# A decoder layer on one core: last batch's end, multiplications of ones in TensorE's waits, half loads, sums on TensorE, and one ring of banks

## The reference

```python
x = x + mla_attention(layernorm(x))     # 16 heads, low-rank q (192) and kv (64), rope of 64, causal
x = x + quantized_expert(layernorm(x))  # SmoothQuant int8 gate/up and down, weights given per batch
x = x + moe(layernorm(x))               # 32 experts, top 4 of 3 of 8 groups, 40 slots each, and a shared expert

def _smooth_quant_linear(x, w):
    s = sqrt(max(amax_x, EPS) / max(amax_w, EPS))        # by column
    x_scale, w_scale = rowmax(|x / s|) / 127, rowmax(|w * s|) / 127
    return round(x / s / x_scale) @ round(w * s / w_scale).T * x_scale * w_scale.T

# moe: a slot is kept when its place in its expert's queue is below C = 40
Yf = Y.reshape(EC, d) * slots_w[:, None]
out = zeros((T, d)).at[slots_token].add(Yf)
```

## Time and profile before

| | |
|---|---|
| median of 3 runs | 391.88 us (391.5 to 392.9) |
| profiled execution | 394.86 us, span 393.0 us, mean clock of TensorE 0.953 |
| TensorE busy | 320.9 us, 82% |
| VectorE busy | 258.6 us, 66% |
| ScalarE busy | 171.5 us, 44% |
| GpSimd busy | 101.3 us, 26% |
| chain that ended last | PE 46%, DVE 22%, issue 12%, ACT 8%, POOL 7%, DMA 4% |

### The profile page before, as it was taken

The page is one execution under the profiler, slowest core; times in us unless marked ns, Lnnn a source line. Parts: engine busy times, 40 slices in busy tenths (PEclk is TensorE's granted clock), DMA queues, the critical chain, the costliest instruction groups (busy, mean ns, idle before and its releaser), DMA issues.

```text
span 393.0 us, 6471 instructions
## 1 busy us (share of the span) xinstructions
PE 320.9 (82%) x1960; PEld 222.9 (57%) x1960; DVE 258.6 (66%) x1058; ACT 171.5 (44%) x536; POOL 101.3 (26%) x144
## 2 busy tenths in 40 slices
PE   1899998899998878998798899777697571699890
PEld 0555665566866656765465676555585461455580
DVE  2347776676488868867897879785596590143527
ACT  1225576756547665336584716654033100134200
POOL 4121222221031102035422014331015416015700
PEclk9999999999999999998999999989989877599996
DMA  7999691020000000000000000153000000545165
GB/s 263 337 407 366 219 387 51 0 81 2 2 2 0 3 1 0 3 5 34 6 3 5 3 0 2 35 181 115 0 2 3 16 2 2 139 133 206 32 239 201
DMA packets 17894, 34.25 MB, mean 87 GB/s; under 512 B 4780, under 2 KB 9513, under 8 KB 17220
## 3 DMA queue, kind: packets, MB, share of 16 engines
q1 hardware_dynamic: 15556, 32.64, 23.7%
q0 software_dynamic: 2304, 1.20, 1.1%
HBM read 27.08 MB, written 11.99 MB: 99 GB/s over the span
## 4 chain that ended last, share of the span: by engine, by line
PE 46%; DVE 22%; issue 12%; ACT 8%; POOL 7%; DMA 4%; POOLq 0%; DVEq 0%; another core or an unknown queue 0%; SPq 0%; ACTq 0%
PE psum L522 37%; PE psum L531 9%; POOL expert_rows L1574 2%; DVE x_residual L1491 2%; DVE region_t L1159 2%; ACT region_t L918 1%; POOL token_parts L1585 1%; ACT region_r L866 1%; DVE region_t L1167 1%; DMA region_a<-token_parts 1%; DMA x_residual<-in_x_dram 1%; ACT region_t L916 1%; DVE region_t L1157 1%; POOL rstd L1536 1%; DVE bn_stats L1057 1%
## 5 line engine op out<-in xcount | busy, mean ns | idle before, releaser
L522 PE MATMUL psum<-region_h,region_b 128*128 128x256 f32 (+1 forms) x320 | 66.9, 347 | 2.9 <-DVE region_b L1471 1.8
L522 PE MATMUL psum<-region_c,region_h 128*128 128x512 f32 x128 | 62.2, 610 | 2.1 <-ACT q_chunk L866 1.1
L916 ACT ACTIVATE region_t<-region_t,neg_max 128x128 f32<-128x128 f32 x64 | 25.6, 401 | 67.3 <-DVE neg_max L1159 65.6
L522 PEld LDWEIGHTS psum<-region_h,region_b 128*128 128x128 f32 x320 | 48.2, 194 | 11.1 <-issue 5.5
L1548 POOL TENSOR_TENSOR q_chunk<-q_chunk,q_rope_tmp 128x256 f32<-128x256 f32 x32 | 23.4, 733 | 97.7 <-DVE q_chunk L1138 97.6
L1574 POOL DMA_INDIRECT expert_rows<-h_moe,slot_scatter x32 | 33.2, 1037 | 24.1 <-DVE slot_scatter L1403 16.2
L531 PE MATMUL psum<-consts,region_t 128*128 128x128 f32 x192 | 32.5, 278 | 7.6 <-DVE region_t L1167 4.5
L522 PEld LDWEIGHTS psum<-region_c,region_h 128*128 128x128 f32 x128 | 23.1, 194 | 20.3 <-issue 17.2
L531 PEld LDWEIGHTS psum<-consts,region_t 128*128 128x128 f32 x192 | 22.9, 142 | 20.4 <-issue 13.0
L918 ACT ACTIVATE region_t<-region_t,neg_max 128x256 f32<-128x256 f32 x64 | 31.6, 494 | 0.0
L522 PE MATMUL psum<-region_t,region_h 128*64 128x256 f32 (+1 forms) x256 | 27.8, 340 | 2.9 <-ACT region_t L866 2.9
(11 more groups left out here) (185 smaller groups left out, 603.5 us busy)
## 6 DMA issues: line engine op xcount, KB each, us to landing
region_a<-in_experts_dram SPq DMA_DIRECT2D x17, 384.0 KB, 6.2
region_b<-in_experts_dram SPq DMA_DIRECT2D x10, 384.0 KB, 6.6
region_a<-in_fold_dram SPq DMA_DIRECT2D x3, 1152.0 KB, 13.2
token_parts<-region_g SPq DMA_DIRECT2D x12, 256.0 KB, 5.8
region_a<-token_parts SPq DMA_DIRECT2D x6, 512.0 KB, 6.2
region_c<-in_experts_dram SPq DMA_DIRECT2D x5, 384.0 KB, 3.2
expert_rows<-region_g SPq DMA_DIRECT2D x10, 132.5 KB, 10.6
region_h<-expert_rows SPq DMA_DIRECT2D x5, 256.0 KB, 3.8
```

What stands on the lines that cost most here:

```text
L522: return nc.tensor.matmul(out_, lhsT, rhs, start=first, stop=last)
L916: nc.scalar.activation(pr[:, 0:P], pr[:, 0:P], ACT.Exp, bias=nmax[:, hn, 0:1], scale=-1.0, accum_out=sums[:, hn, 0:1])
```

## The change

- `FILL`: TensorE multiplies a 128x128 bf16 matrix of ones by itself, into the bank of the step that follows, 20 times before x_T.3, 30 before x_back.3, 40 before x_back2.3, 140 before xpT.0. The wait for the empty bank comes first; the wait for the data comes behind the ones. The rows of the last batch are still scattered and loaded.
- The end: each tile's parts are loaded in two halves (256 KB), even tiles by SyncE, odd tiles by ScalarE; stores are divided in the same way. Tiles 4 and 5 are no longer combined on VectorE: `weigh` makes 8 matrices, the identity times a token weight, and `sum` multiplies them with the parts on TensorE, four f32 matmuls of 128x256 a tile; VectorE adds the sum to the residual.
- `inv_ready` comes in two halves, xs and then ws, and `x_back` has 6 parts and not 4.
- The `q` projections lose their own bank; the ring of the attention stage is banks 4 to 7 for all.
- The whole `ORDER` is written anew. Up to `tail` the same steps stand in a similar order; behind it the part below.

```diff
-BANK_S, BANK_PT, BANK_O, BANK_Q, BANK_W = 0, 2, 3, 4, 5
+BANK_S, BANK_PT, BANK_O, BANK_W = 0, 2, 3, 4
+FILL = {("x_T", 3): 20, ("x_back", 3): 30, ("x_back2", 3): 40, ("xpT", 0): 140}
 ORDER, from the step behind `tail` on, new:
+y_first.7 tail y_last.6 y_last.7 y_add.6 y_add.7 x_stats.3 x_stats.3+1 r_logit.2 r_groups.2 r_groups.2+1
+r_groups.2+2 x_norm.3 r_groups.2+3
+r_groups.2+4 r_groups.2+5 r_best.2 x_T.3 x_T.3+1 r_best.2+1 r_best.2+2 r_best.2+3 r_best.2+4 r_best.2+5
+x_smooth.3 x_smooth.3+1 r_choose.2 r_choose.2+1 r_choose.2+2 x_smooth.3+2 r_choose.2+3 r_weights.2 s_gate.0
+s_up.0 s_silu.0 r_weights.2+1 x_scale.3 x_back.3 r_weights.2+2 r_weights.2+3 x_back.3+1 r_weights.2+4 s_mul.0
+s_gate.1 x_back.3+2 x_back.3+3 x_back.3+4 s_down.0 r_weights.2+5 r_pos.2 x_back.3+5 s_silu.1 x_qscale.3
+x_round.3 x_qT.3 scatter.2.0 r_slots.2 r_slots.2+1 r_slots.2+2 r_slots.2+3 x_mm.3 x_tanh.3 r_slots.2+4 x_gate.3
+s_up.1 x_gate.3+1 x_gate.3+2 x_gate.3+3 x_smooth2.3 x_smooth2.3+1 x_smooth2.3+2 x_scale2.3 scatter.2.1
+scatter.2.2 x_back2.3 scatter.2.3 scatter.2.4 scatter.2.5 x_back2.3+1 x_back2.3+2 s_add.0 s_mul.1 x_qscale2.3
+s_gate.2 x_round2.3 x_qT2.3 x_mm2.3 x_mm2.3+1 x_mm2.3+2 s_down.1 scatter.2.6 scatter.2.7 r_stats.3 r_stats.3+1
+s_add.1 r_norm.3 s_silu.2 s_up.2 s_mul.2 r_T.3 r_logit.3 r_groups.3 r_groups.3+1 r_groups.3+2 r_groups.3+3
...
+scatter.3.0 s_down.3 xpT.0 scatter.3.1 scatter.3.2 s_add.2 s_mul.3 xpT.1 s_add.3 gate_up.0 scatter.3.3
+scatter.3.4 scatter.3.5 scatter.3.6 gate_up.1 gate_up.2 hidT.0 hidT.1 xpT.2 xpT.3 scatter.3.7 slot_weights
+down.0 gate_up.3 gate_up.4 hidT.2 hidT.3 down.1 down.2 gate_up.5 onehot.0 xpT.4 hidT.4 down.3 gate_up.6 down.4
+hidT.5 gate_up.7 onehot.1 onehot.2 onehot.3 onehot.4 onehot.5 onehot.6 onehot.7 down.5 hidT.6 down.6 hidT.7
+down.7 onehot.8 onehot.9 onehot.10 onehot.11 onehot.12 onehot.13 onehot.14 onehot.15 weigh.0 combine.0 mix.6
+combine.2 mix.7 sum.4 sum.5
@@ SyncE
-            for t in range(SCATTERED):
-                sp.dma_start(parts[:, t, :], pv[t]).then_inc(ld_parts[t], 16)
+            for t in range(0, SCATTERED, 2):
+                for half in range(2):
+                    c0 = half * TOPK * D // 2
+                    sp.dma_start(parts[:, t, c0:c0 + TOPK * D // 2], pv[t][:, c0:c0 + TOPK * D // 2]
+                                 ).then_inc(ld_parts[half][t], 16)
@@ TensorE
+            def busy(item, n):
+                for _ in range(n):
+                    mm(bank(item)[:, 0:P], ones_bf[:], ones_bf[:])
...
+                    wait_empty(pe, step)
+                    busy(step, FILL.get(step, 0))
                     pe.wait_ge(ld_rows[i], 16)
...
+                elif kind == "sum":
+                    t, = a
+                    pe.wait_ge(sg["weigh_ready"], 1)
+                    wait_empty(pe, step)
+                    for k in range(TOPK):
+                        if k % 2 == 0:
+                            pe.wait_ge(ld_parts[k // 2][t], 16)
+                        last = mm(bank(step)[:, 0:D], weigh[:, SUMMED.index(t), k, :], parts[:, t, k * D:(k + 1) * D],
+                                  k == 0, k == TOPK - 1)
+                    fills(last, step)
@@ VectorE
+                elif kind == "weigh":
+                    dve.wait_ge(sg["token_weights_ready"], B)
+                    wait_filled(dve, ("dn", NG_E - 1))
+                    for i, t in enumerate(SUMMED):
+                        for k in range(TOPK):
+                            last = v.tensor_scalar(weigh[:, i, k, :], ident, wtok[:, t, k:k + 1], None, ALU.mult)
+                    last.then_inc(sg["weigh_ready"], 1)
```

More of the change, by code:

```diff
@@ L100 @@
[L100 to L114, removed]
@@ L145 @@
-s_gate.0 x_scale.3 r_choose.2+3 r_weights.2 r_weights.2+1 r_weights.2+2 s_up.0 s_silu.0 x_back.3 x_back.3+1
-r_weights.2+3 r_weights.2+4 x_back.3+2 x_back.3+3 x_qscale.3 r_weights.2+5 r_pos.2 scatter.2.0 s_gate.1 s_mul.0
-r_slots.2 x_round.3 r_slots.2+1 r_slots.2+2 s_down.0 s_add.0 x_qT.3 x_mm.3 r_slots.2+3 r_slots.2+4 x_tanh.3
-x_gate.3 x_gate.3+1 x_gate.3+2 x_gate.3+3 s_silu.1 x_smooth2.3 x_smooth2.3+1 x_smooth2.3+2 s_up.1 s_mul.1
-scatter.2.1 scatter.2.2 scatter.2.3 scatter.2.4 s_gate.2 x_scale2.3 scatter.2.5 scatter.2.6 x_back2.3
@@ L150 @@
-x_back2.3+1 x_back2.3+2 s_down.1 x_qscale2.3 x_round2.3 s_silu.2 s_add.1 x_qT2.3 x_mm2.3 scatter.2.7 x_mm2.3+1
-x_mm2.3+2 r_stats.3 s_up.2 r_stats.3+1 r_norm.3 r_T.3 r_logit.3 s_mul.2 r_groups.3 r_groups.3+1 r_groups.3+2
-s_down.2 r_groups.3+3 r_groups.3+4 r_groups.3+5 r_best.3 r_best.3+1 r_best.3+2 r_best.3+3 r_best.3+4 r_best.3+5
-r_choose.3 r_choose.3+1 r_choose.3+2 r_choose.3+3 r_weights.3 r_weights.3+1 r_weights.3+2 r_weights.3+3 s_gate.3
-r_weights.3+4 r_weights.3+5 r_pos.3 r_slots.3 r_slots.3+1 r_slots.3+2 r_slots.3+3 r_slots.3+4 s_up.3 s_silu.3
@@ L155 @@
-scatter.3.0 s_down.3 s_mul.3 s_add.2 s_add.3 scatter.3.1 scatter.3.2 scatter.3.3 scatter.3.4 scatter.3.5
-scatter.3.6 xpT.0 xpT.1 gate_up.0 xpT.2 scatter.3.7 gate_up.1 hidT.0 gate_up.2 hidT.1 down.0 slot_weights xpT.3
-gate_up.3 hidT.2 down.1 gate_up.4 hidT.3 down.2 xpT.4 gate_up.5 hidT.4 down.3 gate_up.6 hidT.5 down.4 onehot.0
-onehot.1 onehot.2 onehot.3 gate_up.7 hidT.6 down.5 onehot.4 onehot.5 onehot.6 onehot.7 hidT.7 down.6 onehot.8
-onehot.9 onehot.10 onehot.11 down.7 onehot.12 onehot.13 onehot.14 onehot.15 combine.0 mix.6 combine.2 mix.7
@@ L196 @@
     "xpT": [("xpT", 1)], "gate_up": [("gu", 1)], "hidT": [("hidT", 1)], "down": [("dn", 1)],
-    "mix": [("mix", 1)],
+    "mix": [("mix", 1)], "sum": [("sum", 1)],
 }
@@ L948, in _ @@
                     b, = a
-                    act.wait_ge(sg["inv_ready"], b + 1)
                     if b >= 1:
```

174 lines of the change are left out of this document (105 added, 69 removed).

## The result

The changed kernel took 400.13 us (median of 4 runs, 398.15 to 401.81) beside 392.39 us for the kernel before (4 runs, 391.5 to 393.52): ratio 1.0194, 95% interval 1.0124 to 1.0263. The forecast was 388.5, range 385.2 to 392.4, so it is wrong in sign; what happened has the place and nearly the size of rival D. The profiled execution took 401.79 us, span 400.0, against 394.86 and 393.0 before.

What follows compares the result with a forecast made beforehand. TensorE bounds attention, a serial chain the last batch's steps, TensorE the experts, then scatters, loads and VectorE the end. Terms -3.0 - 1.0 + 0.9 - 0.4 - 0.3 + 0.4 = -3.4 from 391.88 gave 388.5 us, range 385.2 to 392.4.

Steps and rivals of the forecast that it cites:

- rival D: Attention: new order sets dependent steps closer and starves TensorE; slower from +5.8 us of gaps, 395 at +7; chance 0.1.
- Attention: 22 to 262 us, shared ring and rewritten order: TensorE's gaps change little, +0.4 us, bounds -3 to +5.
- the other terms: All but attention: end -3.0, ones -1.0, cross step +0.9, router -0.4, experts' order -0.3 us.
- pairs of probsT: Attention: pairs with nothing between them cost 0.74 us each and rise from 5 to 7.
- q's wait: Attention: the separate bank of q cost one wait of 1.1 us, which can go.
- The end: Combine and sum: half loads and TensorE sums let VectorE end at 387.7, not 390.79; -3.0 us, bounds -1.3 to -4.0.
- The 140 ones: Before xpT.0: ones end about 3 us before the rows and partly save the experts' clock; -1.0 us, bounds 0 to -2.5.
- Cross step and router: Last batch: moved steps and ones outweigh clock gains in the cross step, +0.9 us; r_logit.3 at full clock, -0.4 us.
- the split of the reciprocals: Cross step: inv_ready in halves should scale xs early, but moved steps intervene; +0.7 us.
- The experts' order: Experts: 14 scatters in a row on GpSimd end at 374.3 against 374.6; -0.3 us, bounds -1 to +1.

Runs made afterwards that it cites:

- the halves: Changed kernel with the order split at x_stats.1, one side as before: old then new 399.68 us (1.0105), new then old 394.08 us (0.999).
- the end alone: Kernel before with half loads from two engines, tiles 4 and 5 summed on TensorE and split reciprocals, no ones: 391.84 us, 0.9965.
- The kernel with new order, then old: Changed kernel with its new order up to x_stats.1 and the order of before behind it, up to the tail: 394.08 us, 0.999.
- the end alone with wide ones: Kernel before with the new end (half loads, TensorE sums, split reciprocals) and 46 ones of 512 columns before xpT.0: 393.47 us, 0.9971.

## Why the prediction was wrong, step by step

**Attention, the step that failed: +0.4 predicted, +6.2 measured, of which some 3.3 at an equal clock.** It is the largest miss but not the only one: with +0.4 in its place the trace would still be 1.2 us late, because the other terms, -3.8 in sum by prediction, came to +0.8. The new order taken out brings the time back to before (1.0016), put in alone it gives a loss as large as that of the whole change (1.0193). The prediction counted TensorE's work between a step and the one that depends on it, and priced the pairs of probsT with nothing between them, which rise from 5 to 7. Those waits (the copy on VectorE, 3.7 us in 7 waits before) fell to 2.5 us in 3. What grew was not priced at all: waits for VectorE's side work (normalised rows L1108 for batches 0 to 2, 3.9 to 7.7 us in the lines of region_r, h_cross and h_moe; the second half of norm, L1189, 0.6 to 2.7; the masks' maximum, L1200, none to 1.4). TensorE's work between two steps is only one side of a distance. The order is also VectorE's own queue, and what lies in that queue between cause and answer was left out. That TensorE's waits for VectorE grew by 6.1 us is shown. That they grew because of what stands ahead in VectorE's queue is argued from the lines waited for, not shown: no pair was moved alone, and the halves say only that there is more than one. x_scaledT was in the prediction (one distance of 3.8 to 3.2 us) and grew from 3.1 us in 2 waits to 4.5 in 4. The gain of q's wait (1.1 us) came, the shared ring as a whole is worth some 2 us by the table, and both are less than the 5.5 us of the order.

Rival D had the place and that TensorE is starved there; its reason, dependent steps set closer together, was counted on TensorE alone like the term. It decided from +5.8 us of gaps, and gaps grew by 5.5, to a time of 400 and not 395, since the end and the ones did not give the 3.8 us that D set against them. Its chance of 0.1 was too low: a rewritten order over 240 us with bounds of -3 to +5 was entered in the sum near zero because signs of single distances went both ways.

**The end: -3.0 predicted, -0.8 measured (1.2 us in the end alone).** The mechanism was right. In the end alone VectorE started at 379.80 (predicted 379.6) and its second round ended at 386.9 (386.6). Mis-sized were the sums. First, a mix of the earlier trace rows is 64 records in 14.08 us, but 32 matmuls: each costs 0.44 us, not 0.22, and the 6 left behind the last half cost 2.87 us (12 records in the chain), not 1.3. Second, the last half lands at 394.46, 10.7 us behind the start of the loads; predicted were 10.0. Issuing from two engines shortened no slow start:

```profile
383.70:386.20 2.50, 2.50 (x14) 2.19 (x12) 0.00 (x0) 0.00 (x0) 0.00 (x0) 1.00 0.37 103
386.20:394.50 8.30, 7.09 (x33) 5.62 (x31) 7.06 (x18) 0.00 (x0) 0.00 (x0) 1.00 1.02 380
```

```profile
375.90:378.40 2.50, 2.50 (x13) 2.19 (x13) 0.00 (x0) 0.00 (x0) 0.00 (x0) 1.00 0.58 131
```

The first fence is of the changed kernel, the second of the kernel before. The first 2.5 us of the loads ran at 103 GB/s, and at 131 before; then the plateau of the earlier trace rows came, at 380. So 1.6 us of the miss are matmuls and 0.7 loads. The Trainium skill (FP8 and Floating Point Precision, "TensorE Precision Notes") says that true FP32 takes four passes through the array. By that rule 256 columns are 1024 at the upper level of the clock, an estimate of 0.43 us, and the 0.44 of the mix agrees.

**The 140 ones: -1.0 predicted, +3.3 of delay measured, 1.7 us got back.** They were priced by the time of a short burst (0.057 us each) and called covered, with 3 us to spare before the rows. Three things moved. They started at 333.7 and not 325.8: 6.0 us of that are attention and router, which move the rows too, and 1.9 are new, most of it s_down.3, which took 3.63 us in place of 1.99, at half clock behind 2.72 us of idle. After 51 ones came three gaps, 2.9 us in sum, with 5 and 4 ones between them, which no wait explains. And the last 80 took 6.25 us and not 4.6, since the clock fell to half behind the gaps. Together that is 6.4 us, against the 3 to spare. The prediction had this price (4.6 us of delay if they ran twice as slow) and set it aside because the clock was full when they began; it did not stay full. Behind them the 8 transposes took 1.04 us and not 2.18 and gate_ups were at full clock, the gain that the prediction bounded at 2.5: 1.7 us up to the last scatter, by the kernel without ones. Without the ones the changed kernel was 2.1 us faster.

**Cross step and router: +0.9 and -0.4 predicted, -0.2 together.** The shared matmuls took 3.62 us and not 5.31 and the 30 ones stood right ahead of x_back.3, both as predicted. From the first maximum (296.10) the scaling starts 2.4 us later, 1.87 before, and qT_bf's copy 4.9 us later, where 5.7 was predicted and 5.02 was before: the split of the reciprocals about pays what the moved steps cost. r_logit.3 took 0.66 us and not 1.07, as predicted, but half clock did not go from this stretch: it came right behind, in 320 to 323.

**The experts' order: -0.3 predicted, +0.2 to +0.8 measured.** onehot.0 now waits on VectorE for down.4 ahead of gate_up.6's work: 6.43 us of VectorE's idle and 1.99 of TensorE's. The prediction had looked only at when the one-hot matrices end, not at what they hold up.

## What to carry to other kernels

Where a change reorders a long list of steps, the distances must be summed on every engine that answers, and not on TensorE alone (here it was the waits for VectorE that grew); where that can't be done, the term is as wide as its bounds and its losing side needs a real chance. Multiplications that only hold the clock must end before the data land: few wide ones, and a count taken from the shortest wait, not the longest; here they were worth 0.3 to 2.4 us at best. Before a difference of two traces is put down to a change, compare the time at half clock in both. Divide a group's time by matmuls, not by records.

## What the runs showed that I had not expected

Long rows of narrow bf16 ones stall. In the traces of all six kernels with 140 of them before xpT.0 the first 51 to 61 run through, then 1 to 5 at a time with gaps of 0.3 to 1.1 us, while GpSimd's scatters of rows are in flight; behind the last scatter 67 to 80 run without a gap. The kernel with new order, then old, timeline of TensorE:

```profile
325.57 3.46 PE L530 MATMUL psum<-ones_bf 128*128 128x128 bf16 x59
329.68 0.44 PE L530 MATMUL psum<-ones_bf 128*128 128x128 bf16 x5 [0.65 <-issue]
331.11 0.34 PE L530 MATMUL psum<-ones_bf 128*128 128x128 bf16 x3 [0.99 <-issue]
...
333.98 5.21 PE L530 MATMUL psum<-ones_bf 128*128 128x128 bf16 x68 [0.45 <-issue]
```

35, 40 and 46 wide ones beside the same scatters had no gap. That fits a limit on instructions, not on columns. A fetch of instructions by DMA is not what they wait for, as far as the views show: the DMA view counts packets of kind "instruction", and in the changed kernel one lies in 326 to 328 us and the next two in 346 to 348, none in the gaps. What they do wait for is in no view, and ones without scatters beside them were not tried.

The clock can be low in the mix. In three profiled executions with the new experts' order the mix took 17 us in place of 14.08, and the sums then had to wait for it; four others of the same order took 14.08, and all with the experts' order of before did. The Trainium skill (TensorE: Matmul & The Clock Gate, Part 1) calls the moment of change run-variable for one kernel; the spread of the runs (390.27 to 395.88 for the end alone with wide ones) fits that, and so do the 3.4 to 13.7 us at half clock in the table, but no run sets it apart from other causes.
